# A routed feed-forward stage on one core: the first layer's fp32 product replaced by three fp32r products of high and low parts

## The chip, the cores and the metric

The kernel runs on one core of a Trainium2 chip. The metric is the device time of one execution in microseconds, lower is better. The kernel before took 1937.72 us in the median of 3 runs (1935.43 to 1938.97).

## The reference, cut to what matters

Four layers in a row, each followed by a residual sum and a layer norm: a linear attention, a switch attention, a rotary attention and, last, a feed-forward layer that works on half of the tokens. The change is in the last one alone:

```python
def _L1_ffn_ref(x, w_r, b_r, W1, b1, W2, b2):   # x (4, 1024, 128), W1 (128, 512), W2 (512, 128)
    k = int(0.5 * s)
    weights = (jnp.einsum('bsd,do->bso', x, w_r) + b_r).squeeze(-1)
    top_vals, _ = jax.lax.top_k(weights, k)
    selected = weights > top_vals[:, -1][:, None]
    hidden = jax.nn.gelu(jnp.einsum('bsd,dh->bsh', x, W1) + b1, approximate=False)
    blk = jnp.einsum('bsh,hd->bsd', hidden, W2) + b2
    return jnp.where(selected[..., None], blk, x)
x = _layernorm(x + _L1_ffn_ref(x, ...), axis=-1)
```

## The kernel before

The last stage is `depth_lead`. It works on four batches (b = 0 to 3) of T = 1024 tokens, each with NT = 8 tiles of 128 tokens. HALF is 512 columns, one PSUM bank. Every engine runs a program of its own, in the order in which it is written, and the engines wait for each other by counting semaphores.

TensorE, for each batch, runs `expand(b, 0)`, then `turn_x(b + 1)` (eight transposes of the next batch's x into two banks), `expand(b, 1)`, `router_row(b + 1)` (the router's product, two halves), `expand(b, 2)`, `expand(b, 3)`, `router_column(b + 1)` (eight tiny transposes), and `contract(b)` (the second layer, 32 products of 128 columns). `expand(b, n)` (line 2588, its product on L2594) computes 128 of the 512 hidden units for 1024 tokens. `turn_x(0)`, `router_row(0)` and `router_column(0)` come ahead of the loop.

ScalarE runs `hidden(b, 0)` (the gelu of 1024 columns, L2529), `copy_x(b + 1)` (two copies PSUM to SBUF, L2511), `hidden(b, 1)`, `copy_rows(b + 1)` (L2522), `hidden(b, 2)`, `hidden(b, 3)`, and then `finish_norm(b - 1)` (eight instructions, L2537), which writes the output of the batch before. So the next batch's `hidden(b + 1, 0)` stands behind `finish_norm(b - 1)`.

VectorE runs `choose(0)` and then, for each batch, `choose(b + 1)`, `gather(b, half)` and `moment_stats` for both halves (L2661, L2669), and `moment_guess(b)` (L2678 to L2681). `choose` counts for every token how many have a router weight at least as large: eight passes over 1024 columns (L2641), then `d_sel` and `d_weight` (L2647, L2649). `moment_guess(b)` waits until `finish_norm(b - 1)` has written all its eight tiles (`dve.wait_ge(normed, NT * b)`), since it overwrites the statistics that those read.

GpSimd runs `keep(b + 1)` (three products and sums over 1024 columns, L2474, L2475, L2477, which wait for `d_weight`) and then `inverse_roots(b)` (14 instructions of 8 columns each, L2486 to L2491, which wait for `d_rs` of L2681). ScalarE's `finish_norm(b)` waits for the last of them. Only for the last batch does VectorE do the roots itself (`last_norm`).

SyncE writes each batch's output when its tiles are there. The weights were loaded in the stage before.

Of the kernel before, what the change touches and what calls it, by code (L numbers as in the profile page):

```python
# [11 lines left out]
F32 = mybir.dt.float32  # L12
F32R = mybir.dt.float32r
BF16 = mybir.dt.bfloat16
I32 = mybir.dt.int32
ALU = mybir.AluOpType
# [3 lines left out]
P = 128  # L20
B, T, D = 4, 1024, 128
NT = T // P
HALF = 512
# [2389 lines left out]
def depth_lead(nc, x, out_dram, ps, ident, I, place, signals, past, weights, kept_from, tag):  # L2413

    FF = 512
    NB = FF // P
    K = T // 2
    ctx = ExitStack()
    with ctx:  # L2419
        sb = lambda name, shape, dt=F32: ctx.enter_context(nc.sbuf_tensor(tag + name, shape, dt))  # L2420
        sem = signals.names(tag)
        w1, w2, b1, b2, wr, br = weights.w1, weights.w2, weights.b1, weights.b2, weights.wr, weights.br
        xT = sb("xT", [P, 2, T])
        w_row, w_col, ge = sb("w_row", [P, 2, T]), sb("w_col", [P, 2, NT]), sb("ge", [P, 2, T])
        count, sel, weight = sb("count", [P, NT]), sb("sel", [P, 2, NT]), sb("weight", [P, 2, NT])
        hid = sb("hid", [P, NB, T])
# [5 lines left out]
        assert kept_from is None or nc.sbuf_base <= kept_from  # L2432
        r_in, w1_in, w2_in, b2_in = weights.r_in, weights.w1_in, weights.w2_in, weights.b2_in
        turned, xT_sb, row_ps, row_sb, col_ps, col_sb = map(sem, ("turned", "xT_sb", "row_ps", "row_sb", "col_ps", "col_sb"))
        hid_ps, hid_sb, blk_ps = map(sem, ("hid_ps", "hid_sb", "blk_ps"))
        counts, chosen, scaled, kept_rdy, y_rdy = map(sem, ("counts", "chosen", "scaled", "kept", "y"))
        moments, newton, normed, norm_steps = map(sem, ("moments", "newton", "normed", "norm_steps"))
        out_done = [sem(f"out_done{b}") for b in range(B)]
        piece_b = [ps[:, 0, :], ps[:, 1, :]]
        hid_b = [ps[:, i:i + 2, :].rearrange("p a n -> p (a n)") for i in (2, 4)]  # L2440
# [21 lines left out]
        @block.gpsimd  # L2462
        def _(pool):
            if past is not None:
                past.clear(pool)

            def keep(b):

                if b == 0:
                    pool.wait_ge(b2_in, 16)  # L2470
                pool.wait_ge(chosen, 2 * b + 2)
                if b >= 2:
                    pool.wait_ge(y_rdy, NT * (b - 1))
                nc.gpsimd.tensor_tensor(kept[:, b % 2, :, :], x[:, b * NT:(b + 1) * NT, :], weight[:, b % 2, :].unsqueeze(2).broadcast_to([P, NT, D]), ALU.mult).then_inc(scaled, 1)  # L2474
                nc.gpsimd.tensor_tensor(shifts[:, :, :], b2[:, :].unsqueeze(1).broadcast_to([P, NT, D]), sel[:, b % 2, :].unsqueeze(2).broadcast_to([P, NT, D]), ALU.mult).then_inc(scaled, 1)  # L2475
                pool.wait_ge(scaled, 2 * b + 2)
                nc.gpsimd.tensor_tensor(kept[:, b % 2, :, :], kept[:, b % 2, :, :], shifts[:, :, :], ALU.add).then_inc(kept_rdy, 1)  # L2477
                pool.wait_ge(kept_rdy, b + 1)

            def inverse_roots(b):  # L2480

                pool.wait_ge(moments, MOMENT_STEPS * (b + 1))
                st = Steps(pool, newton, NEWTON_STEPS * b)
                var, half_step = tmp[:, 0, :], tmp[:, 1, :]
                for _ in range(3):
                    st.link(nc.gpsimd.tensor_tensor(half_step, rs[:, :], rs[:, :], ALU.mult))  # L2486
                    st.link(nc.gpsimd.tensor_tensor(half_step, half_step, var, ALU.mult))
                    st.link(nc.gpsimd.tensor_scalar(half_step, half_step, -0.5, 1.5, ALU.mult, ALU.add))
                    st.link(nc.gpsimd.tensor_tensor(rs[:, :], half_step, rs[:, :], ALU.mult))
                st.link(nc.gpsimd.tensor_tensor(shift[:, :], mv[:, :, 0], rs[:, :], ALU.mult))  # L2490
                st.done(nc.gpsimd.tensor_scalar(shift[:, :], shift[:, :], -1.0, None, ALU.mult))  # L2491
                assert st.n == NEWTON_STEPS, st.n

            keep(0)
            for b in range(B):
                if b + 1 < B:
                    keep(b + 1)
                    inverse_roots(b)

        @block.scalar  # L2500
        def _(act):
            nc.scalar.preload_act_table(ACT.Gelu)

            def copy_x(b):

                for half in range(2):
                    act.wait_ge(turned, 2 * b + half + 1)
                    if b >= 2 and half == 0:
                        act.wait_ge(hid_ps, NB * (b - 1))
                    cols = slice(half * HALF, (half + 1) * HALF)  # L2510
                    nc.scalar.copy(xT[:, b % 2, cols], piece_b[half]).then_inc(xT_sb, 1)  # L2511

            def copy_rows(b):

                if b == 0:
                    act.wait_ge(r_in, 16 * 2)
                if b >= 2:
                    act.wait_ge(counts, NT * (b - 1))
                for half in range(2):
                    act.wait_ge(row_ps, 2 * b + half + 1)  # L2520
                    cols = slice(half * HALF, (half + 1) * HALF)
                    nc.scalar.activation(w_row[:, b % 2, cols], piece_b[half], ACT.Identity, bias=br[:, 0:1]).then_inc(row_sb, 1)  # L2522

            def hidden(b, n):

                act.wait_ge(hid_ps, NB * b + n + 1)
                if b and n == 0:
                    act.wait_ge(blk_ps, 2 * b)
                nc.scalar.activation(hid[:, n, :], hid_b[n % 2], ACT.Gelu, bias=b1[:, n:n + 1]).then_inc(hid_sb, 1)  # L2529

            def finish_norm(b):

                act.wait_ge(newton, NEWTON_STEPS * (b + 1))
                if b >= 2:
                    act.wait_ge(out_done[b - 2], 16)
                for t in range(NT):
                    nc.scalar.activation(yo[:, b % 2, t, :], y[:, b % 2, t, :], ACT.Identity, bias=shift[:, t:t + 1], scale=rs[:, t:t + 1]).then_inc(normed, 1)  # L2537

            copy_x(0)
            copy_rows(0)  # L2540
            act.wait_ge(w1_in, 16 * 2)
            for b in range(B):
                hidden(b, 0)
                if b + 1 < B:
                    copy_x(b + 1)
                hidden(b, 1)
                if b + 1 < B:
                    copy_rows(b + 1)
                hidden(b, 2)
                hidden(b, 3)  # L2550
                if b:
                    finish_norm(b - 1)
            act.wait_ge(norm_steps, 10)
            act.wait_ge(out_done[B - 3], 16)
            for t in range(NT // 2, NT):
                nc.scalar.activation(yo[:, (B - 1) % 2, t, :], y[:, (B - 1) % 2, t, :], ACT.Identity, bias=shift[:, t:t + 1], scale=rs[:, t:t + 1]).then_inc(normed, 1)  # L2556

        @block.tensor
        def _(pe):
# [12 lines left out]
            def router_row(b):  # L2572

                if b == 0:
                    pe.wait_ge(r_in, 16 * 2)
                for half in range(2):
                    pe.wait_ge(xT_sb, 2 * b + half + 1)
                    nc.tensor.matmul(piece_b[half], wr[:, :], xT[:, b % 2, half * HALF:(half + 1) * HALF], start=True, stop=True).then_inc(row_ps, 1)  # L2578

            def router_column(b):  # L2580
# [6 lines left out]
            def expand(b, n):  # L2587

                if NB * b + n >= 2:
                    pe.wait_ge(hid_sb, NB * b + n - 1)  # L2590
                if b == 0 and n == 0:
                    pe.wait_ge(w1_in, 16 * 2)
                for s in range(0, T, HALF):
                    last = nc.tensor.matmul(hid_b[n % 2][:, s:s + HALF], w1[:, n * P:(n + 1) * P], xT[:, b % 2, s:s + HALF], start=True, stop=True)  # L2594
                last.then_inc(hid_ps, 1)

            def contract(b):
# [28 lines left out]

        @block.vector
        def _(dve):

            def choose(b):  # L2630

# [52 lines left out]
            def last_norm(b):  # L2684
# [11 lines left out]
                for t in range(NT // 2):  # L2696
                    st.done(nc.vector.tensor_scalar(yo[:, b % 2, t, :], y[:, b % 2, t, :], mv[:, t, 0:1], rs[:, t:t + 1], ALU.subtract, ALU.mult))

            choose(0)
            for b in range(B):  # L2700
                if b + 1 < B:
                    choose(b + 1)
                st = Steps(dve, moments, MOMENT_STEPS * b)
                for half in range(2):
                    gather(b, half)
                    moment_stats(b, st, half)
                moment_guess(b, st)
# [87 lines left out]
def program(nc, I, out_dram):  # L2795
    ctx = ExitStack()
    with ctx:
# [7 lines left out]
        with ExitStack() as held:  # L2805
# [31 lines left out]

            linear.release()
            depth_lead(nc, r3, out_dram, ps, ident, I, nc.Block(), depth, middle, weights, lead.kept_from, "d_")
            middle.release()  # L2840
        redo_all(nc, r1, r2, out_dram, ps, ident, I, depth, flag)
# [81 lines left out]
```

## Time and profile before

| what | value |
|---|---|
| median of 3 runs | 1937.72 us |
| the profiled execution | 1932.66 us, span 1930.9 us |
| last stage | from 1836.8 us to the end of the span |
| TensorE busy | 1739.3 us, 90% of the span |
| VectorE, ScalarE, GpSimd busy | 1136.8, 1274.8, 939.5 us |
| mean granted TensorE clock | 0.966 |

Times in the trace count from the start of the span. "PE" is TensorE's product, "PEld" its weight load, DVE is VectorE, ACT is ScalarE, POOL is GpSimd. A product in plain fp32 appears as two instructions. Ends of products are modelled, so their pace is read from their starts.

### The profile page before, as it was taken

How to read it: one execution, taken by the hardware profiler on the slowest of the kernel's cores; microseconds unless marked ns; L12 is line 12 of the kernel's file. 1: busy time of each engine (PE TensorE's matmuls, PEld its weight loads, DVE VectorE, ACT ScalarE, POOL GpSimd, SP SyncE). 2: the span in 40 equal slices, each digit the busy share in tenths (PEclk: the TensorE clock that was granted, in tenths of full speed). 3: DMA queues.
4: the chain of work that ended last, by engine and by line, in shares of the span. 5: the costliest groups of instructions: out<-in, count | busy, mean ns of one | idle time of the engine just before them, and what ended most of it. 6: DMA issues, size and time to landing. Idle time of an engine off the chain costs nothing. (4 is left out here: it accounts for less than half of the span.)

```text
span 1930.9 us, 25433 instructions
## 1 busy us (share of the span) xinstructions
PE 1739.3 (90%) x8942; PEld 832.9 (43%) x8942; DVE 1136.8 (59%) x1868; ACT 1274.8 (66%) x2447; POOL 939.5 (49%) x566
## 2 busy tenths in 40 slices
PE   7888479999999999999999999879999999998695
PEld 3443345545554445554454555324333333332264
DVE  5888597986668876588766566531423223120286
ACT  2121215766767677767577666768998999999543
POOL 3556206778876778757798678860000000000033
PEclk9999689999999999999999999989999999999898
DMA  2000100000000000000000000130221312201001
GB/s 72 1 1 0 35 11 11 21 21 11 21 11 22 11 21 11 22 11 21 11 22 20 12 11 11 33 131 23 66 88 31 123 40 70 74 36 36 1 12 35
DMA packets 27863, 59.04 MB, mean 31 GB/s; under 512 B 3840, under 2 KB 14800, under 8 KB 27728
## 3 DMA queue, kind: packets, MB, share of 16 engines
q1 hardware_dynamic: 27728, 57.32, 9.2%
q8 instruction: 75, 1.23, 0.3%
q14 instruction: 60, 0.49, 0.1%
HBM read 38.44 MB, written 18.87 MB: 30 GB/s over the span
## 5 line engine op out<-in xcount | busy, mean ns | idle before, releaser
L742 POOL TENSOR_TENSOR b_psum<-b_psum,b_probs 128x1024 f32<-128x1024 f32 x192 | 461.5, 2404 | 181.1 <-ACT b_probs L886 174.9
L2193 ACT ACTIVATE c_probs<-banks 128x1024 f32<-128x1024 f32 x512 | 483.5, 1029 | 46.0 <-PE banks L2242 35.1
L1268 DVE TENSOR_TENSOR b_gated<-banks,b_g 128x480 f32<-128x480 f32 x512 | 314.2, 655 | 229.4 <-PE banks L987 224.5
L886 ACT ACTIVATE b_probs<-banks 128x1024 f32<-128x1024 f32 x256 | 254.0, 1018 | 226.5 <-PE banks L1020 225.7
L987 PE MATMUL banks<-b_w,b_xh 128*128 128x480 f32 x1024 | 353.9, 400 | 32.7 <-DVE b_gated L1268 18.6
L1276 DVE TENSOR_REDUCE b_tok<-b_gated 128x192 f32<-128x960 f32 x256 | 281.3, 1138 | 0.5
L1020 PE MATMUL banks<-b_qq,b_kk 64*128 64x512 f32 x1024 | 262.2, 623 | 10.2 <-DVE b_gated L1268 10.0
L857 ACT ACTIVATE b_share<-b_o,b_picked 128x64 f32<-128x64 f32 x1080 | 268.7, 337 | 1.5 <-DVE b_o L1301 1.5
L1052 PE MATMUL banks<-b_probs,b_tok 128*64 128x512 f32 x1024 | 252.2, 614 | 2.2 <-ACT b_probs L886 2.2
L2257 PE MATMUL banks<-c_probs,c_vg 128*32 128x512 f32 x2048 | 249.4, 605 | 2.9 <-DVEq L2300 2.6
L987 PEld LDWEIGHTS banks<-b_w,b_xh 128*128 128x128 f32 x1024 | 195.2, 191 | 115.6 <-issue 40.0
L2178 POOL COPY c_vg<-c_v 128x64 f32<-128x64 f32 x60 | 12.8, 255 | 424.5 <-PE banks L2257 376.2
L2242 PE MATMUL banks<-c_queries,c_keys 32*128 32x512 f32 x1024 | 193.0, 465 | 27.0 <-ACT c_probs L2193 26.0
L987 PE MATMUL banks<-b_w,b_xl 128*128 128x480 f32 x512 | 196.3, 383 | 0.0
L2242 PEld LDWEIGHTS banks<-c_queries,c_keys 32*128 32x128 f32 x1024 | 79.8, 183 | 195.3 <-ACT c_probs L2193 174.9
L753 POOL TENSOR_TENSOR b_z<-b_z,b_share 128x1280 f32<-128x1280 f32 x54 | 157.5, 2917 | 0.0
L1052 PEld LDWEIGHTS banks<-b_probs,b_tok 128*64 128x64 f32 x1024 | 62.7, 137 | 175.9 <-issue 143.5
L1020 PEld LDWEIGHTS banks<-b_qq,b_kk 64*128 64x128 f32 x1024 | 87.5, 187 | 106.6 <-issue 54.5
L304 POOL TENSOR_TENSOR a_qscan<-a_scan,a_q 128x1024 f32<-128x1024 f32 x36 | 89.9, 2497 | 88.4 <-DVE a_scan L467 88.2
L742 POOL TENSOR_TENSOR b_psum<-b_probs 128x1024 f32<-128x1024 f32 x32 | 76.4, 2387 | 78.1 <-ACT b_probs L886 78.1
L2257 PEld LDWEIGHTS banks<-c_probs,c_vg 128*32 128x32 f32 x2048 | 53.8, 110 | 117.7 <-issue 78.8
L2347 DVE COPY c_acc<-banks 128x512 f32<-128x512 f32 x32 | 22.1, 691 | 138.4 <-PE banks L2257 137.5
(243 smaller groups left out, 1877.0 us busy)
## 6 DMA issues: line engine op xcount, KB each, us to landing
b_raw_w<-in_L_ffn_W SPq DMA_DIRECT2D x32, 480.0 KB, 3.4
c_heads<-c_split SPq DMA_DIRECT2D x24, 512.0 KB
c_keys<-c_heads SPq DMA_DIRECT2D x16, 512.0 KB, 3.6
c_queries<-c_heads SPq DMA_DIRECT2D x16, 512.0 KB, 4.6
c_heads<-c_split SPq DMA_DIRECT2D x8, 384.0 KB
a_xs<-in_L_attn_x SPq DMA_DIRECT2D x4, 512.0 KB, 8.0
out<-d_yo SPq DMA_DIRECT2D x3, 512.0 KB, 3.6
c_heads<-c_split SPq DMA_DIRECT2D x8, 128.0 KB
```

The source lines that it names most:

```text
L742: nc.gpsimd.tensor_tensor(psum[:, par, :], prev, probs[:, i % 4, :], ALU.add).then_inc(psum_rdy, 1)
L753: nc.gpsimd.tensor_tensor(zf, zf, sf, ALU.add).then_inc(z_rdy[half], 1)
L857: nc.scalar.activation(dst[:, e, :], o[:, t, :], ACT.Copy, scale=picked[:, b % 2, t, h * E + e:h * E + e + 1]).then_inc(share_rdy, 1)
L886: nc.scalar.activation(probs[:, i % 4, :], score_b[i % 2], ACT.Exp).then_inc(exp_rdy, 1)
L987: last = nc.tensor.matmul(proj_b[u % WAYS][:, 0:HALF_W], a[:, x_of % 2, t * P:(t + 1) * P], w[:, par, part, j, :], start=(i == 0), stop=(i ...
L1020: last = nc.tensor.matmul(score_b[i % 2][:, lo:hi], kk[rows, par, (side + i) % 2, i // 2 * P:(i // 2 + 1) * P], qq[rows, par, :], start=Tr ...
L1052: last = nc.tensor.matmul(acc_b[DH * half:DH * half + DH, :], tok[:, n % 4, 2, i, :], probs[:, i % 4, lo:hi], start=(i == 0), stop=(i == N ...
L1268: nc.vector.tensor_tensor(shape(gated[:, t % 2, j, :]), shape(proj_b[u % WAYS][:, 0:HALF_W]), g.unsqueeze(2).broadcast_to([P, 3, HD2, E]), ...
L1276: nc.vector.tensor_reduce(tok[:, n % 4, :, t, :].rearrange("p j (f d) -> p f j d", f=2), gated[:, t % 2, :, :].rearrange("p f (j d e) -> p ...
L2193: nc.scalar.activation(probs[:, step % 4, c, :, :], unit_b[u % NU], ACT.Exp, scale=float(HD) ** -0.5).then_inc(exp_rdy, 1)
L2242: last = nc.tensor.matmul(unit_b[u % NU][:, s, :], keys[at:at + 32, par, kt * P:(kt + 1) * P], queries[at:at + 32, par, c * HALF:(c + 1) * ...
L2257: last = nc.tensor.matmul(acc_b[at:at + 32, :], vg[par][:, kt, 2 * pp + s, :], probs[:, kt % 4, half, s, :], start=(kt == 0), stop=(kt == ...
```

## The change

ScalarE makes a second copy of each transposed half, rounded to fp32r (`xh`), behind the plain copy `xT`, which the router and VectorE still use. VectorE makes `xl = xT - xh` in a new step `split_low(b)`, two instructions of 512 columns, ahead of `choose(b)`. The weights are split once: `w1h` by ScalarE ahead of `copy_rows(0)`, `w1l` by GpSimd ahead of `keep(0)`. `expand` does three fp32r products in place of the fp32 one, for each of its two halves. New waits: `router_row` for `x_high`, `expand(b, 0)` for `x_low` (and once for `w_low`), ScalarE's `copy_x(b)` from b = 2 for `x_low` of batch b - 2, `split_low(b)` from b = 2 for the products of batch b - 2.

```diff
+        xh, xl = sb("xh", [P, 2, T], F32R), sb("xl", [P, 2, T], F32R)
+        w1h, w1l = sb("w1h", [P, NB * P], F32R), sb("w1l", [P, NB * P], F32R)
...
+            pool.wait_ge(w_high, 1)
+            nc.gpsimd.tensor_tensor(w1l[:, :], w1[:, :], w1h[:, :].bitcast(F32), ALU.subtract).then_inc(w_low, 1)
             keep(0)
...
                     if b >= 2 and half == 0:
                         act.wait_ge(hid_ps, NB * (b - 1))
+                        act.wait_ge(x_low, 2 * (b - 1))
                     cols = slice(half * HALF, (half + 1) * HALF)
                     nc.scalar.copy(xT[:, b % 2, cols], piece_b[half]).then_inc(xT_sb, 1)
+                    nc.scalar.copy(xh[:, b % 2, cols], piece_b[half]).then_inc(x_high, 1)
...
             copy_x(0)
+            act.wait_ge(w1_in, 16 * 2)
+            nc.scalar.copy(w1h[:, :], w1[:, :]).then_inc(w_high, 1)
             copy_rows(0)
-            act.wait_ge(w1_in, 16 * 2)
...
                     pe.wait_ge(xT_sb, 2 * b + half + 1)
+                    pe.wait_ge(x_high, 2 * b + half + 1)
                     nc.tensor.matmul(piece_b[half], wr[:, :], xT[:, b % 2, half * HALF:(half + 1) * HALF], start=True, stop=True).then_inc(row_ps, 1)
...
                 if b == 0 and n == 0:
-                    pe.wait_ge(w1_in, 16 * 2)
+                    pe.wait_ge(w_low, 1)
+                if n == 0:
+                    pe.wait_ge(x_low, 2 * b + 2)
                 for s in range(0, T, HALF):
-                    last = nc.tensor.matmul(hid_b[n % 2][:, s:s + HALF], w1[:, n * P:(n + 1) * P], xT[:, b % 2, s:s + HALF], start=True, stop=True)
+                    for i, (w, a) in enumerate(((w1h, xh), (w1h, xl), (w1l, xh))):
+                        last = nc.tensor.matmul(hid_b[n % 2][:, s:s + HALF], w[:, n * P:(n + 1) * P], a[:, b % 2, s:s + HALF], start=(i == 0), stop=(i == 2))
...
+            def split_low(b):
+
+                if b >= 2:
+                    dve.wait_ge(hid_ps, NB * (b - 1))
+                for half in range(2):
+                    cols = slice(half * HALF, (half + 1) * HALF)
+                    dve.wait_ge(x_high, 2 * b + half + 1)
+                    nc.vector.tensor_tensor(xl[:, b % 2, cols], xT[:, b % 2, cols], xh[:, b % 2, cols].bitcast(F32), ALU.subtract).then_inc(x_low, 1)
...
+            split_low(0)
             choose(0)
             for b in range(B):
                 if b + 1 < B:
+                    split_low(b + 1)
                     choose(b + 1)
```

## Rows read from the trace of the kernel before

**Rows 1.** The chain of waits, last stage: start, duration, engine, tile, line
```profile
1842.98 1.91 PE banks L2594 x4
1861.31 1.72 PE banks L2594 x4
1897.47 6.88 PE banks L2594 x16
1905.54 7.43 PE banks L2608 x64
1912.99 1.13 DVE d_y L2661 x4
1915.05 0.65 DVE d_mv L2678 x8
```

**Rows 2.** One full batch: busy PE, PEld, DVE, ACT, POOL, granted clock, DMA, GB/s
```profile
1861.15:1879.20 18.05, 17.43 (x102) 12.23 (x101) 16.59 (x46) 9.87 (x16) 8.93 (x17) 1.00 0.05 13
```

**Rows 3.** Timeline of VectorE, last stage: start, duration, ..., idle before and releaser
```profile
1853.14 0.17 DVE L2649 TENSOR_SCALAR d_weight<-d_sel 128x8 f32<-128x8 f32 x1
1853.25 0.17 DVE L2633 COPY d_w_col<-banks 128x8 f32<-128x8 f32 x1
1871.39 0.17 DVE L2633 COPY d_w_col<-banks 128x8 f32<-128x8 f32 x1 [1.19 <-PE banks L2584]
1889.47 0.17 DVE L2633 COPY d_w_col<-banks 128x8 f32<-128x8 f32 x1 [1.29 <-PE banks L2584]
1906.09 0.17 DVE L2681 TENSOR_SCALAR d_rs<-d_tmp 128x8 int32<-128x8 int32 x1
```

**Rows 4.** Timeline of GpSimd, last stage
```profile
1853.47 1.90 POOL L2474 TENSOR_TENSOR d_kept<-c_r,d_weight 128x1024 f32<-128x1024 f32 x1 [98.84 <-DVE d_weight L2649]
1906.40 0.20 POOL L2486 TENSOR_TENSOR d_tmp<-d_rs 128x8 f32<-128x8 f32 x1 [0.38 <-DVE d_rs L2681]
1910.07 0.23 POOL L2491 TENSOR_SCALAR d_shift<-d_shift 128x8 f32<-128x8 f32 x1
```

**Rows 5.** Timeline of ScalarE, last stage
```profile
1838.11 1.31 ACT L2511 COPY d_xT<-banks 128x512 f32<-128x512 f32 x2
1840.78 1.49 ACT L2522 ACTIVATE d_w_row<-banks,c_d_br 128x512 f32<-128x512 f32 x2 [1.37 <-PE banks L2578]
1864.08 1.06 ACT L2511 COPY d_xT<-banks 128x512 f32<-128x512 f32 x2
1892.26 3.19 ACT L2537 ACTIVATE d_yo<-d_y,d_shift,d_rs 128x128 f32<-128x128 f32 x8 [2.26 <-POOL d_shift L2491]
1899.22 1.11 ACT L2529 ACTIVATE d_hid<-banks,c_d_b 128x1024 f32<-128x1024 f32 x1 [3.77 <-PE banks L2594]
1910.34 3.19 ACT L2537 ACTIVATE d_yo<-d_y,d_shift,d_rs 128x128 f32<-128x128 f32 x8 [4.85 <-POOL d_shift L2491]
```

**Rows 6.** Timeline of TensorE, switch attention: fp32r products of 480 columns
```profile
902.20 0.59 PE L987 MATMUL banks<-b_w,b_xh 128*128 128x480 f32 x2
902.63 0.38 PE L987 MATMUL banks<-b_w,b_xl 128*128 128x480 f32 x1
```

**Rows 7.** Timelines, switch attention: a split of x by ScalarE and VectorE
```profile
225.33 1.13 ACT L827 CAST b_xh<-b_xT 128x512 fp32r<-128x512 f32 x2
226.05 1.29 DVE L1213 TENSOR_TENSOR b_xl<-b_xT,b_xh 128x512 fp32r<-128x512 f32 x2 [10.47 <-ACT b_xh L827]
```

**Rows 8.** Timelines of VectorE and GpSimd where both read SBUF
```profile
367.26 3.27 DVE L1232 TENSOR_TENSOR b_beats<-b_gate 128x256 bf16<-128x256 f32 x2
367.33 2.69 POOL L742 TENSOR_TENSOR b_psum<-b_psum,b_probs 128x1024 f32<-128x1024 f32 x1
```

**Rows 9.** Groups by line and shape: GpSimd, whole span and last stage
```profile
L742 POOL TENSOR_TENSOR b_psum<-b_probs 128x1024 f32<-128x1024 f32 x32 | 76.4, 2387 | 78.1 <-ACT b_probs L886 78.1
L2477 POOL TENSOR_TENSOR d_kept<-d_kept,d_shifts 128x1024 f32<-128x1024 f32 x4 | 9.4, 2350 | 0.3
```

**Rows 10.** Stretches and TensorE's timeline around a gap: the granted clock stands behind POOL's busy time
```profile
675.87 1.58 PE L1020 MATMUL banks<-b_qq,b_kk 64*128 64x512 f32 x4 [3.29 <-DVE b_gated L1268]
676.40:679.90 3.50, 3.50 (x10) 0.77 (x8) 1.53 (x2) 2.41 (x8) 1.31 (x1) 0.51 0.00 0
```

More of the change, by code:

```diff
@@ L2434, in depth_lead @@
         turned, xT_sb, row_ps, row_sb, col_ps, col_sb = map(sem, ("turned", "xT_sb", "row_ps", "row_sb", "col_ps", "col_sb"))
+        x_high, x_low, w_high, w_low = map(sem, ("x_high", "x_low", "w_high", "w_low"))
         hid_ps, hid_sb, blk_ps = map(sem, ("hid_ps", "hid_sb", "blk_ps"))
```

## The prediction

> **What bounds the kernel now.** I read the chain of waits first, cut to the last stage, since nothing before it is touched. There the chain runs on TensorE almost without a break: a batch's blocks, then its contraction, one batch after the other, from 1842.98 us to 1912.99 us [rows 1]. Four fp32 instructions of one block (two halves) start 1.72 us apart in all (0.43 us each). Only then does it pass to VectorE, whose last stretch begins with the means of batch 3 at 1915.05 us. That view names a single bound, and it tempts one to price the change by TensorE alone. So I read the stretch of one full batch next: of 18.05 us TensorE is busy 17.43 and VectorE 16.59 [rows 2]. VectorE's own timeline shows what is left: between one batch's `d_rs` and the next `choose` it is idle 1.19 us and 1.29 us, waiting for the router's columns [rows 3]; between batch 0 and batch 1 it is not idle at all (its `d_weight` at 1853.14 is followed by the next copy at 1853.25). VectorE's round is thus only 1.2 us shorter than TensorE's, and the change shortens the one and lengthens the other.
>
> The third reading is what hangs on VectorE's round. When `d_rs` of batch 2 is there at 1906.26, GpSimd runs its 14 root instructions to 1910.30 [rows 4] and ScalarE `finish_norm(2)` from 1910.34 to 1913.53 [rows 5]. `moment_guess(3)` on VectorE waits for exactly that (`normed >= 24`), and begins at 1915.05 because its own statistics came later. So this second path ends 1.52 us ahead of the first; with some 0.07 us for the semaphore, it has 1.45 us of slack.
>
> **TensorE's part.** An fp32r product of 480 columns starts every 0.215 us (902.20 to 902.63 for two) [rows 6]. For 512 columns I take 0.215 to 0.23 us; the weights are loaded alongside there as they will be here. A block goes from 1.72 us to 6 x 0.215 = 1.29 us, so 0.43 us less, 1.7 us in a batch, 6.9 us in all. Part of it goes back at once: the router now waits for both copies of each half. Two copies take 1.06 us [rows 5], four 2.12. In a batch's time, block 0 ends at 1.3, the gelu at 2.6, the four copies at about 4.75; the router's second half starts then, 0.5 us later than TensorE could, and the gelu of block 3 ends at 9.7 (10.8 before). A batch of TensorE becomes about 17.0 us (18.05 before). In the last batch nothing but blocks and gelus is left: gelu 1.11 us plus about 0.3 of hand-over against 1.29 per block and two banks, about 1.4 us per block, 1.5 us less in all. If TensorE alone set the end, the gain would be 3 x 1.0 + 1.5 = 4.5 us.
>
> **VectorE's path, which I take to set the end.** Five terms.
>
> Start. `choose(0)` waits for rows that wait for the router, now behind `xh`. The plain copies end at 1839.42; four take about 1.1 us more, `w1h` 0.55 more (a cast SBUF to SBUF, two in 1.13 us [rows 7]). But the router's products were the late ones: ScalarE was idle 1.37 us for them ahead of the rows [rows 5]. The first half of the router starts 0.5 us later, partly regained as its second pass falls beyond the rise of the clock. I take +0.3 us. Bounds: +0.1 (all hidden) to +1.6 (all three copies in series). The `w1l` subtraction of GpSimd, half of a 2.35 us instruction [rows 9], about 1.2, ends near 1842.4, ahead of the first block; if that cover is gone it costs the first block a few tenths, on TensorE alone. `split_low(0)` lies in VectorE's idle time ahead of `choose(0)`.
>
> `split_low(1)`. Two subtractions of 512 columns take 1.29 us, 0.6 us apart [rows 7]. This pair follows `d_weight` of batch 0 at once, and GpSimd's first `keep` instruction starts 0.22 us after that point (1853.47 against 1853.25) [rows 3, 4]. What happens when a VectorE instruction with two SBUF inputs meets a GpSimd instruction is in the trace: a pair of small comparisons took 3.27 us, while a GpSimd instruction began 0.07 us after the first, took 2.69 us and ended at 370.02, half a microsecond before the pair [rows 8] (it takes 2.39 us in the mean of its like [rows 9]). So the first comparison ran, GpSimd waited for it, then GpSimd ran whole, and only then the second comparison. Here the same gives 0.6 (first half) + 1.9 (GpSimd's product [rows 4]) + 0.6 (second half) = 3.1 us. Bounds: 1.2 (the pair goes through) and 5.0 (GpSimd also gets ahead of the first). I take 3.1, as the row is this very case.
>
> The Trainium skill says the same in "SBUF — State Buffer", section "SBUF: two separate sides": the pair of ports that VectorE and GpSimd share is locked for a whole instruction by whichever starts first, and the other blocks fully. By that rule the first half starts first and the rest depends on who comes next; [rows 8] decide for GpSimd, and read otherwise the rule would leave this term at 1.2.
>
> `split_low(2)` and `split_low(3)` follow `d_rs`, when GpSimd starts its roots, instructions of 0.2 us. Each pair costs 1.2 plus at most one or two such instructions: 1.3 us each (1.2 to 1.6). GpSimd is held up in turn by about 0.7 us, which delays `finish_norm(0)` and `finish_norm(1)`, not `finish_norm(2)`, beside which no split runs.
>
> What comes back: the idle 1.19 and 1.29 us, since the router's columns come earlier than VectorE is ready: 2.5 us.
>
> Sum for `d_rs` of batch 2: 0.3 + 3.1 + 2 x 1.3 - 2.5 = +3.5 us, at 1909.8. Roots and `finish_norm(2)` follow as before, ending at 1917.0; 3.5 less the slack of 1.45 leaves about +2.0 us for the start of the means of batch 3, and behind these nothing changes.
>
> Does TensorE's path stay below? `finish_norm(1)` comes 3.6 + 0.7 us later (1892.26 + 4.3, ending near 1899.8), and the gelu of block 0 of batch 3 is behind it, at 1899.9 (1899.22 before). From there to the contraction 5.4 us (6.3 before): 1905.3, and the statistics of batch 3 end 0.2 us earlier than before, at 1914.8. That is 2.2 us ahead of 1917.0. The contraction's other condition, `gather(2)`, comes at 1900.9 + 3.5 = 1904.4. The `x_low` wait of `expand(b, 0)` is met: `split_low(2)` ends near 1874.9 and `split_low(3)` near 1893.1, against blocks due from 1877.4 and 1895 on.
>
> **Forecast.** The profiled execution took 1932.66 us (span 1930.9); with the sum 1934.7. The median of the runs is 5.1 us above the profiled one, and I add the sum to the median: 1939.7 us. All 6.9 us that TensorE is spared go into waiting.
>
> **Rivals.** (A) The pair of `split_low(1)` is not parted by GpSimd: 0.3 + 1.2 + 2.5 - 2.5 - 1.45 = 0, so 1937.7. For it: each of the second halves is ready to issue before the first ends. Against: the parted pair in [rows 8]. Chance 0.22.
>
> (B) TensorE's path sets the end after all and gains 4.5 us: 1933.2. It needs VectorE's path not to lengthen; the wait for `normed` stands in the code and its slack is 1.45 us, and even without any port wait this path eats it. Chance 0.04.
>
> (C) TensorE's clock. In batch 2 the copies stand behind a `finish_norm(0)` that ends near 1881, so TensorE waits some 3 us for the router. After a gap of 3.29 us the trace shows 3.5 us at a granted clock of 0.51, the level of 1.2 GHz [rows 10]. Such a fall in batch 2 costs 1.7 us, mostly covered by ScalarE's lateness; a second that meets the contraction of batch 3 (7.4 us at full clock [rows 1]) costs 1.7 to 7.4 more. It decides once the contraction ends over 2.2 us late: at 5 us late the time is 1942.5, with the contraction wholly at half clock 1944.9. For it: the waits grow. Against: ahead of the last contraction I see no gap of that length, and at gaps of 0.7 us the clock stayed at 1.00 [rows 2]. Chance 0.12.
>
> My forecast has 0.62. A difference of 0.2%, 3.9 us, is about what a measurement of this kernel can tell from no change. Faster by more: 0.04, case B. Slower by more: C, and the upper end of the forecast (a start near 1.6 or a parted first half), 0.16. The same: 0.80. By the bounds the path gives -0.3 (0.1 + 1.2 + 2.4 - 2.5 - 1.45) to +5.9 us (1.6 + 5.0 + 3.2 - 2.5 - 1.45); cutting the far end and allowing 1.5 us for the scatter of medians, the range is 1936.0 to 1943.0.
>
> **What would show each step.** In the profile after: fp32r starts 0.21 to 0.23 us apart; the first subtraction of `split_low(1)` about 0.7 us and the second about 2.4, with a `keep` instruction between; VectorE without idle time before `choose(2)` and `choose(3)`; the means of batch 3 released by ScalarE's `d_yo` and not by the statistics; idle time of TensorE before the router's product. If the chain of waits still runs over the contraction of batch 3, the sum is wrong in its main choice; if the second subtraction takes 0.7 us, it is rival A.

## The result and the profile after

Timed in 20 runs each, the changed kernel takes 1940.08 us in the median (1934.61 to 1947.31) and the kernel before 1936.20 (1931.16 to 1941.36); the ratio is 1.0022, 95% interval 1.0012 to 1.0032. By that ratio it is slower by 4.3 us (2.3 to 6.2); the medians differ by 3.9. A second set of 11 runs, beside 34 of the kernel before, gave 1.0027 (1.0017 to 1.0036). The forecast was 1939.7 us within 1936 to 1943.

The stages ahead of the last one are the same instructions in every kernel here, yet in the 14 profiles the last one begins anywhere between 1834.70 and 1846.56 us after the start of the span. Ahead of it TensorE had its low clock for 105.7 us in the earliest profile and for 129.4 us in the latest. So the mechanism is read inside the last stage, counted from ScalarE's table load, which begins it (1839.18 us in the profile after). From there to the end it took 94.05 and 94.25 us in two profiles of the kernel before, 97.85 and 97.78 us in two of the changed one: +3.7 us.

The chain of waits of the changed kernel, last stage: start, duration, engine, tile, line. (The dots stand for lines that are left out.)

```profile
1841.70 3.77 PE banks L2587 x4
...
1847.48 9.70 DVE d_ge L2662 x16
...
1858.09 2.38 DVE d_xl L2649
1860.58 9.70 DVE d_ge L2662 x16
...
1875.31 1.74 DVE d_tmp L2701
1877.15 0.48 DVE d_xl L2649
...
1916.59 0.20 POOL d_shift L2493
...
1917.54 2.79 ACT d_yo L2544 x7
1920.45 0.31 DVE d_mv L2699 x3
```

Where [rows 1] showed a TensorE that never left the chain, the chain now enters VectorE with the first `choose` and stays there until the `d_rs` of batch 2, goes over GpSimd's roots and ScalarE's `finish_norm(2)`, and comes back to VectorE at the means of batch 3. No contraction is on it.

VectorE's timeline of the same kernel, which answers to [rows 3]:

```profile
1847.28 0.17 DVE L2654 COPY d_w_col<-banks 128x8 f32<-128x8 f32 x1 [4.02 <-PE banks L2593]
...
1857.48 2.99 DVE L2649 TENSOR_TENSOR d_xl<-d_xT,d_xh 128x512 fp32r<-128x512 f32 x2
1860.40 0.15 DVE L2654 COPY d_w_col<-banks 128x8 f32<-128x8 f32 x1
...
1877.15 1.30 DVE L2649 TENSOR_TENSOR d_xl<-d_xT,d_xh 128x512 fp32r<-128x512 f32 x2
1878.37 0.15 DVE L2654 COPY d_w_col<-banks 128x8 f32<-128x8 f32 x1
...
1896.28 0.15 DVE L2654 COPY d_w_col<-banks 128x8 f32<-128x8 f32 x1
...
1912.89 0.17 DVE L2702 TENSOR_SCALAR d_rs<-d_tmp 128x8 int32<-128x8 int32 x1
...
1920.45 0.88 DVE L2699 BATCH_NORM_AGGREGATE d_mv<-d_stats 128x2 f32<-128x6 f32 x8 [2.62 <-ACT d_yo L2544]
```

The idle times ahead of the copies of batches 2 and 3 are gone, and a new one of 2.62 us stands ahead of the means, put down to ScalarE's `d_yo`: the wait for `normed`. GpSimd's and ScalarE's timelines, which answer to [rows 4, 5]:

```profile
1857.72 2.20 POOL L2477 TENSOR_TENSOR d_kept<-c_r,d_weight 128x1024 f32<-128x1024 f32 x1 [13.34 <-DVE d_weight L2670]
1859.89 2.34 POOL L2478 TENSOR_TENSOR d_shifts<-c_d_b,d_sel 128x1024 f32<-128x1024 f32 x1
```

```profile
1899.87 3.19 ACT L2544 ACTIVATE d_yo<-d_y,d_shift,d_rs 128x128 f32<-128x128 f32 x8 [6.64 <-POOL d_shift L2494]
1902.97 2.10 ACT L2536 ACTIVATE d_hid<-banks,c_d_b 128x1024 f32<-128x1024 f32 x2
1917.14 3.18 ACT L2544 ACTIVATE d_yo<-d_y,d_shift,d_rs 128x128 f32<-128x128 f32 x8 [8.85 <-POOL d_shift L2494]
```

And here is what the products cost, in TensorE's timeline. Their starts are 0.23 us apart.

```profile
1891.01 0.39 PE L2606 MATMUL banks<-d_xh,d_w1l 128*128 128x512 f32 x1
1891.24 0.39 PE L2606 MATMUL banks<-d_xh,d_w1h 128*128 128x512 f32 x1
1891.46 0.39 PE L2606 MATMUL banks<-d_xl,d_w1h 128*128 128x512 f32 x1
1891.69 0.39 PE L2606 MATMUL banks<-d_xh,d_w1l 128*128 128x512 f32 x1
```

### The profile page after: what moved, and what is told of

Its sections match the earlier page's. It is cut to its first block and busy times, and to the rows that moved or that the text cites. A ratio compares the mean times of both kernels' runs of the same rounds, so it can differ in the third digit from the quotient of the medians.

```text
span 1937.0 us, 25527 instructions
## 1 busy us (share of the span) xinstructions
PE 1736.7 (90%) x8974; PEld 839.8 (43%) x8974; DVE 1147.6 (59%) x1876; ACT 1278.2 (66%) x2456; POOL 943.3 (49%) x567
```

## The experiments

All marks are in us from the start of the last stage, one profile each. "Rise" is when TensorE's granted clock goes from 1.2 to 2.4 GHz, "copy 0" VectorE's first column copy, "copy 1" the second, "rs 2" the guess of the roots of batch 2, "means 3" the first mean of batch 3. "End" is the end of the span. The ratio is to the kernel before, timed beside it.

| kernel | rise | copy 0 | copy 1 | rs 2 | means 3 | end | ratio (95%) |
|---|---|---|---|---|---|---|---|
| before | 3.55 | 6.20 | 16.44 | 69.28 | 78.24 | 94.05 | |
| e12_before_again | 3.88 | 6.37 | 16.61 | 69.44 | 78.41 | 94.25 | 1.0012 (0.9986 to 1.0039) |
| after | 10.89 | 8.09 | 21.21 | 73.71 | 81.27 | 97.85 | 1.0022 (1.0012 to 1.0032) |
| e10_after_again | 6.42 | 7.74 | 20.85 | 73.37 | 80.93 | 97.78 | 1.0027 (1.0017 to 1.0036) |
| e1_high_from_copy | 3.55 | 6.20 | 19.33 | 71.84 | 79.42 | 95.90 | 1.0044 (1.0027 to 1.0061) |
| e8_high_from_copy_again | 3.71 | 6.28 | 19.41 | 71.91 | 79.47 | 96.27 | 1.0018 (1.0006 to 1.0031) |
| e2_low_before_weight | 6.87 | 7.74 | 19.15 | 71.81 | 79.40 | 96.08 | 1.0018 (1.0008 to 1.0029) |
| e3_double_stats | 6.96 | 7.74 | 20.86 | 73.41 | 79.13 | 95.56 | 1.0007 (0.9993 to 1.0020) |
| e4_all_three | 3.91 | 6.39 | 17.80 | 70.46 | 75.44 | 91.78 | 0.9984 (0.9967 to 1.0001) |
| e11_all_three_again | 3.86 | 6.36 | 17.78 | 70.44 | 75.41 | 92.21 | 0.9990 (0.9981 to 1.0000) |
| e5_before_double_stats | 6.29 | 7.24 | 17.48 | 70.32 | 79.29 | 95.49 | 0.9994 (0.9979 to 1.0009) |
| e6_no_low_of_x | 14.01 | 8.08 | 19.81 | 70.65 | 78.39 | 94.98 | 1.0005 (0.9988 to 1.0022) |
| e7_split_fp32_products | 13.94 | 8.09 | 21.26 | 74.13 | 83.11 | 99.81 | 1.0026 (1.0007 to 1.0046) |
| e9_roots_on_gpsimd | 3.96 | 6.40 | 17.82 | | 74.30 | 89.54 | 0.9972 (0.9961 to 0.9984) |

The kernel before, timed against itself, came out at 1.0012 (0.9986 to 1.0039). So a ratio alone does not carry a microsecond here, while the marks of two profiles of one kernel agree within 0.4 us, and only the rise moves further.

**The late start.** `e1_high_from_copy` makes `xh` from `xT` instead of from PSUM, so the router's product waits for the plain copies alone, as before the change:

```diff
                     nc.scalar.copy(xT[:, b % 2, cols], piece_b[half]).then_inc(xT_sb, 1)
-                    nc.scalar.copy(xh[:, b % 2, cols], piece_b[half]).then_inc(x_high, 1)
+                for half in range(2):
+                    act.wait_ge(xT_sb, 2 * b + half + 1)
+                    cols = slice(half * HALF, (half + 1) * HALF)
+                    nc.scalar.copy(xh[:, b % 2, cols], xT[:, b % 2, cols]).then_inc(x_high, 1)
...
-                    pe.wait_ge(x_high, 2 * b + half + 1)
```

> xh is made from xT in SBUF, behind both plain copies, so the router's product no longer waits for it. Times below count from the start of the stage (ScalarE's table load). Theory (the 0.5 us gap ahead of the first router product let TensorE's clock rise late, 10.8 us into the stage instead of 3.6): the rise is back near 3.6 us, VectorE's first column copy starts at about 6.5 us (8.10 in the changed kernel, 6.20 before), and the means of batch 3 start 1.4 to 1.7 us earlier. Rival (the time of the rise has nothing to do with that gap): the copy starts near 7.6 and the means 0.5 us earlier. Whole time about 1.6 us under the changed kernel, some 2 us over the one before.

Copy 0 is back at 6.20 us and the means come 1.85 us earlier. In TensorE's timeline of this kernel the router follows the transposes at once and takes 2.71 us as before:

```profile
1834.74 1.94 PE L2580 MATMUL banks<-ident,c_r 128*128 128x128 f32 x8 [8.02 <-PEq L2837]
1836.72 2.71 PE L2589 MATMUL banks<-d_xT,c_d_wr 128*128 128x512 f32 x4
```

In the changed kernel it waits 0.53 us for `d_xh` and then takes 3.75:

```profile
1839.22 1.94 PE L2577 MATMUL banks<-ident,c_r 128*128 128x128 f32 x8 [8.01 <-PEq L2835]
1841.70 3.75 PE L2587 MATMUL banks<-d_xT,c_d_wr 128*128 128x512 f32 x4 [0.53 <-ACT d_xh L2518]
```

The busy times of two stretches of the changed kernel show why: the granted clock (third from the end) was 0.50, the level of 1.2 GHz, for the whole start of the stage, and 1.00 behind it.

```profile
1839.20:1850.00 10.80, 9.47 (x27) 5.84 (x28) 4.08 (x8) 5.21 (x8) 1.26 (x1) 0.50 0.00 0
1850.00:1865.60 15.60, 14.88 (x103) 12.39 (x102) 15.50 (x26) 7.45 (x10) 6.88 (x3) 1.00 0.00 1
```

The 1.9 us by which copy 0 is late in the changed kernel are thus 0.5 us of waiting, 1.05 us of the router's slower passes and 0.36 us of the eight tiny transposes behind the rows, which took 1.02 us where they took 0.66 before. But the timed runs of e1 came out long: their median was 1943.54 us, 7.4 us above the kernel before, and the profiled run was the shortest of the five. So it ran again, beside the changed kernel itself.

> The same kernel as e1_high_from_copy, whose profile had the stage 1.95 us shorter than the changed kernel's while its timed runs were 7 us above the kernel before. Theory (the timed runs were scatter from the stages ahead, where the clock falls at other places in every execution): 1 to 2 us over the kernel before and 1 to 3 under the changed kernel of the same call; the clock's rise again between 3.5 and 6.5 us into the stage. Rival (the edit costs something that its profile did not show): again more than 4 us over the kernel before.

> The changed kernel unaltered, beside the others on the same chip, and with a second profile. Theory (the router's wait for xh lets the clock rise late): the rise lies again later than 6.5 us into the stage, the first column copy at 7.7 us or later, the means of batch 3 at 80.9 to 81.3. Rival (the late rise was chance): rise near 3.6 us and first column copy near 6.7.

> The kernel before, unaltered, for a second profile of the same start. Theory (without the wait for xh the clock rises early): the rise within 6.5 us of the stage's start, the first column copy at 6.2 to 7.3 us, the means of batch 3 at 78.2 to 79.3. Rival (the time of the rise is chance in either kernel): a rise at 6.9 us or later and a first column copy at 7.7 or later.

The marks of e8 repeat those of e1 within 0.1 us, but for the rise (0.2 us) and the end (0.4 us). In time the expectation for e8 failed: it was 3.7 us over the kernel before and not 1 to 2, and only 0.6 us under the changed kernel timed beside it. Its ratio of 1.0018 and the 1.0027 of the changed kernel cannot be told apart, so the gain of this edit is shown inside the stage alone (96.27 us against 97.78). The 1.0044 of e1 was not met again. The four long runs of e1 had a mean granted clock of 0.960 to 0.963, against 0.967 in the profiled one; what lowered it is not known. Of the expectation for e10, the number 6.5 us for the rise failed by 0.1 (6.42), copy 0 and the means came as written. For e12 all three numbers did. Over all profiles: where the router waits for `xh` (after, e10, e2, e3, e6, e7) the rise lies at 6.42 to 14.01 us and copy 0 at 7.74 to 8.09; where it does not (the other eight) the rise lies at 3.55 to 3.96 and once at 6.29, and copy 0 at 6.20 to 6.40 and once at 7.24. The rise is not fixed in either group. That the gap of half a microsecond delays it is the likeliest reading of 14 profiles, and e5 shows that a late rise also comes without the gap. With nearly the same rise (6.29 us in e5, 6.42 in e10) copy 0 differs by 0.50 us, which is the wait alone; the rest of the late start comes from the clock.

**The parted pair.** `e2_low_before_weight` puts `split_low(1)` ahead of the instructions that release GpSimd:

```diff
                     dve.wait_ge(scaled, 2 * (b - 1))
+                if b == 0:
+                    split_low(1)
                 nc.vector.tensor_scalar(sel[:, b % 2, :], count[:, :], float(K), None, ALU.is_lt).then_inc(chosen, 1)
...
                 if b + 1 < B:
-                    split_low(b + 1)
+                    if b:
+                        split_low(b + 1)
                     choose(b + 1)
```

> split_low(1) stands ahead of d_sel and d_weight of batch 0, so GpSimd has not yet been released. Theory (the shared port parts the pair): its second subtraction takes 0.7 us instead of 2.4, the pair costs 1.2 us instead of 2.9, and the means of batch 3 start 1.6 to 1.8 us earlier than in the changed kernel. Rival (the 2.9 us has another source, such as the copy it reads): nothing changes. Whole time about 1.7 us under the changed kernel.

VectorE's timeline of this kernel:

```profile
1852.53 1.29 DVE L2649 TENSOR_TENSOR d_xl<-d_xT,d_xh 128x512 fp32r<-128x512 f32 x2
1853.74 0.17 DVE L2670 TENSOR_SCALAR d_sel<-d_count 128x8 f32<-128x8 f32 x1
```

The pair takes 1.29 us instead of 2.99. GpSimd's first product, released only now, takes 1.90 us instead of 2.20:

```profile
1854.27 1.90 POOL L2477 TENSOR_TENSOR d_kept<-c_r,d_weight 128x1024 f32<-128x1024 f32 x1 [14.19 <-DVE d_weight L2672]
```

From copy 0 to copy 1 it is 11.41 us, 13.12 in the changed kernel: 1.71 us. Of these 1.5 us arrive at the means, which come 1.87 us earlier, 0.35 of it by the start. GpSimd's product between the two subtractions is the cause of the 2.38 us. The durations fit the exclusive use that the forecast priced: GpSimd's product waited 0.3 us for the first subtraction, and the second subtraction waited for the whole product.

**The wait for the norm.** `e3_double_stats` gives `mv`, `rs`, `shift` and `tmp` two buffers, indexed by `b % 2`:

```diff
-                if b:
-                    dve.wait_ge(newton, NEWTON_STEPS * b)
-                    dve.wait_ge(normed, NT * b)
+                if b >= 2:
+                    dve.wait_ge(newton, NEWTON_STEPS * (b - 1))
+                    dve.wait_ge(normed, NT * (b - 1))
                 for t in range(NT):
-                    st.done(nc.vector.bn_aggr(mv[:, t, :], stats[:, t, :]))
+                    st.done(nc.vector.bn_aggr(mv[:, b % 2, t, :], stats[:, t, :]))
```

> mean, root, shift and scratch have two buffers, so moment_guess(b) waits for the norm of batch b - 2 instead of b - 1. Theory (in the changed kernel the end hangs on finish_norm(2)): the means of batch 3 start right behind the statistics, 2.5 us earlier than in the changed kernel, and the chain of waits runs over the contraction of batch 3 again. Rival (the contraction comes as late anyway): less than 0.5 us. Whole time 2.5 us under the changed kernel, about 1.4 over the one before.

`e5_before_double_stats` is the same edit on the kernel before.

> The kernel before, with two buffers for the statistics. Theory (there the wait for finish_norm(2) had 1.5 us of slack): no change, within 0.3 us in the stage. Rival (that wait costs in both kernels): up to 2.5 us faster.

In e3 the means stand right behind the statistics. They come 2.1 us earlier (1.8 counted from copy 0), and the chain of waits again runs over the contraction, directly behind batch 2's:

```profile
1891.19 7.41 PE banks L2620 x64
1898.60 5.66 PE banks L2606 x24
1904.28 1.12 ACT d_hid L2536
1905.45 7.42 PE banks L2620 x64
...
1914.97 0.65 DVE d_mv L2699 x8
```

In e5 copy 0 came 1.04 us later than before (a late rise) and the means 1.05 us later: the edit itself gives nothing there. The wait costs only where the change made it late. In e3 the forecast's rival C also showed itself. TensorE waited 1.96 us for `xh` in batch 2, behind a late `finish_norm(0)`, and the clock fell. The four router instructions took 3.60 us, and the granted clock of the stretch was 0.60:

```profile
1883.60 3.60 PE L2587 MATMUL banks<-d_xT,c_d_wr 128*128 128x512 f32 x4 [1.96 <-ACT d_xh L2518]
```

```profile
1884.00:1888.00 4.00, 4.00 (x8) 1.81 (x7) 3.88 (x16) 2.81 (x4) 2.93 (x2) 0.60 0.08 22
```

The wait alone does not decide it. In e10 the same wait was 1.89 us, and in e1 and e8 (for `xT`) 2.04 us, and there the clock did not fall:

```profile
1886.13 2.06 PE L2587 MATMUL banks<-d_xT,c_d_wr 128*128 128x512 f32 x4 [1.89 <-ACT d_xh L2518]
```

The contraction of batch 3 starts at 69.6 us in e3, 0.8 us later than in e10, which has the same copy 0: that is what is missing to the 2.5 us expected.

**All three.** `e4_all_three` joins the edits of e1, e2 and e3.

> All three edits. Theory: the means of batch 3 then start where the contraction of batch 3 lets them. VectorE's d_rs of batch 2 comes about 1.1 us later than before the change, gather(2) likewise, the contraction of batch 3 starts near 66 us into the stage (68.7 before), and the means of batch 3 at about 75.5 us (78.24 before, 81.27 in the changed kernel): 2.5 us faster than the kernel before. Rival (the three are one cost seen three times): no more than the best of them alone, some 2.5 us under the changed kernel and over the one before.

> The same kernel as e4_all_three, timed in more rounds, to tell it from the kernel before. Theory: 2.5 us (0.13%) faster than before, in the stage 2.0 to 3.0 us shorter. Rival (its gain was scatter): no difference within 0.5 us.

The means came at 75.44 and 75.41 us, 2.8 and 3.0 us ahead of the two profiles before, and the stage is 1.8 to 2.5 us shorter. In time they gave 0.9984 and 0.9990, just at the edge of what can be told from 1 (2.0 us in the medians of e11, 2.5 expected). Counted from the changed kernel the edits add up roughly: 1.85, 1.5 and 1.8 (the last two without the start, which e1 has) make 5.15 us, and 5.83 were found. The rival, one cost seen three times, is refuted.

**TensorE's side.** In `e6_no_low_of_x` nothing subtracts, the waits for `x_low` are gone or wait for `x_high`, and the second product takes `xh` once more, so its result leaves out the low part of x:

```diff
-                    for i, (w, a) in enumerate(((w1h, xh), (w1h, xl), (w1l, xh))):
+                    for i, (w, a) in enumerate(((w1h, xh), (w1h, xh), (w1l, xh))):
```

> The changed kernel without VectorE's subtractions: the second product takes xh again in place of xl, so the low part of x is left out of the result; all else stands. Theory (VectorE's extra work and the late first column copy are all that stands against the cheaper products): the start stays 1.9 us late, the rest of TensorE's path gains 3 x 0.9 + 1.5 us, and the means of batch 3 start 1.5 to 2.5 us earlier than before the change, 5 us earlier than in the changed kernel. Rival (VectorE's round was as long as TensorE's anyway): the end is VectorE's round again, about +1.9 - 2.5 - 1.5, which is 0 to 2 us under the kernel before.

In `e7_split_fp32_products` all splits and waits stay and the product is the old one:

```diff
-                    for i, (w, a) in enumerate(((w1h, xh), (w1h, xl), (w1l, xh))):
-                        last = nc.tensor.matmul(hid_b[n % 2][:, s:s + HALF], w[:, n * P:(n + 1) * P], a[:, b % 2, s:s + HALF], start=(i == 0), stop=(i == 2))
+                    last = nc.tensor.matmul(hid_b[n % 2][:, s:s + HALF], w1[:, n * P:(n + 1) * P], xT[:, b % 2, s:s + HALF], start=True, stop=True)
```

> The changed kernel with all its splits and waits, but the product itself stays the plain fp32 one. Theory (VectorE's path sets the end, not TensorE): TensorE's products are 6 us longer in sum, yet less than 1.5 us of it shows against the changed kernel. Rival (TensorE's path would set the end but for the cheaper products): 3 to 5 us slower than the changed kernel.

Both had the latest rise of all, at 14 us. e6 did not do what I wrote: its means came at 78.39, as before the change, 2.9 us ahead of the changed kernel's and not 5. Its chain of waits runs over TensorE, so the mechanism holds, but the start took more than 1.9 us: copy 0 is 1.9 us late, and copy 1 another 1.5 (11.73 us behind copy 0, 10.24 before), since the first blocks ran at 1.2 GHz. Contraction 0 starts 3.4 us later than before, and the 3.2 us that TensorE gains from there to contraction 3 only make up for that. From contraction 0 to 1 and from 1 to 2 it is 17.05 and 17.08 us (18.05 and 18.08 before), the 1.0 us per batch of the forecast.

e7 has its means at 83.11, 1.84 us behind the changed kernel's, a little over my 1.5, and its chain runs over TensorE:

```profile
1912.07 6.88 PE banks L2605 x16
1918.98 1.12 ACT d_hid L2536
1920.14 7.43 PE banks L2619 x64
...
1929.66 0.65 DVE d_mv L2698 x8
```

`finish_norm(2)` ended at 81.56 there, so VectorE's path alone would have given about 81.7, an estimate from that end and the 0.13 us that follow it in the changed kernel. The cheaper products are thus worth 1.4 to 1.8 us inside the changed kernel, after such a start: with the old ones TensorE bounds it, with the new ones VectorE does. After an earlier rise the old products would come earlier too, and what the new ones are worth then was not run.

**A version that beats both.** A wait for GpSimd costs VectorE something in the kernel before too. `d_tmp` (8 columns, 0.17 us in the last batch, beside no `keep`) takes 1.74 us, until GpSimd's last `keep` instruction has ended:

```profile
1868.26 1.74 DVE L2680 TENSOR_SCALAR d_tmp<-d_mv 128x8 f32<-128x8 f32 x1
1867.62 2.35 POOL L2477 TENSOR_TENSOR d_kept<-d_kept,d_shifts 128x1024 f32<-128x1024 f32 x1
```

On top of e4, `e9_roots_on_gpsimd` moves these two instructions to GpSimd, and the splits of batches 2 and 3 into the middle of `choose`:

```diff
+                st.link(nc.gpsimd.tensor_scalar(var, mv[:, b % 2, :, 1], LN_EPS, None, ALU.add))
+                st.link(nc.gpsimd.tensor_scalar(rs[:, b % 2, :].bitcast(I32), var.bitcast(I32), -0.5, float(0x5F3759DF), ALU.mult, ALU.add))
                 for _ in range(3):
...
                 for t in range(NT):
+                    if t == 2 and b >= 2:
+                        split_low(b)
```

(VectorE makes the two for the last batch alone.)

> On top of e4_all_three: d_tmp and d_rs of batches 0 to 2 are made by GpSimd instead of VectorE, where d_tmp stood 1.6 us for GpSimd's last keep instruction, and split_low(2) and split_low(3) stand behind the second pass of choose(2) and choose(3). Theory (the port wait of d_tmp is 1.4 us of VectorE's round): the column copies of choose(2) and choose(3) come 17.0 us apart instead of 17.9, TensorE's path is the bound, and the means of batch 3 start near 74.3 us into the stage (75.44 in e4): about 1 us faster than e4. Rival (another VectorE instruction stands there for the port): the spacing stays near 17.9 and nothing is gained.

The means come at 74.30 us, as written. The copies of batches 2 and 3 are 17.2 us apart, the latter with 1.14 us of idle time ahead of it, put down to the router's columns. The chain of waits is TensorE's again:

```profile
1889.53 1.12 ACT d_hid L2541
1890.70 7.41 PE banks L2624 x64
1898.11 5.64 PE banks L2610 x24
1903.78 1.12 ACT d_hid L2541
1904.94 7.43 PE banks L2624 x64
```

Time: 1930.03 us, 1936.22 before, ratio 0.9972 (0.9961 to 0.9984), the only one here clearly under the kernel before. Of the 4.5 us by which its stage is shorter, 3.9 lie ahead of the means; the other 0.6 lie in the tail behind them, whose cause is open. Which of its two edits does how much was not separated.

## Why the prediction was right

The mechanism was as forecast, and the time of 1940.08 us lies 0.4 us from the forecast 1939.7. That closeness is partly luck. The forecast was 2.0 us of added path on a base of 1937.72 us, the median of 3 runs; over 20 runs the kernel before takes 1936.20, 1.5 us less. The change itself cost 3.9 to 4.3 us, about twice what the sum said. Two terms were too small, the start and the stretch behind the means, and smaller errors the other way hid part of that.

**Start.** Taken as +0.3 us, bounds 0.1 to 1.6; found +1.9, outside the bounds, and, in the second pair of profiles, +1.4. This is the term that was mis-sized most. I priced the wait as a shift of half a microsecond and reckoned that the clock would rise when it had before. In all six profiles with that wait it rose only behind the router. The router's passes then start 0.85 us apart to the last, where before the change the last of them started 0.43 us apart.

**`split_low(1)`.** Taken as 3.1, found 2.88 (copy 0 to copy 1: 13.12 and 13.11, before 10.24), and e2 shows the cause. The first subtraction took 0.68 us and the second 2.38, with GpSimd's product between them.

**`split_low(2)`, `split_low(3)`.** Taken as 1.3 each, found 1.22 from the first subtraction to the next copy. The first starts 0.08 us behind the start of `d_rs`, so from `d_rs` to the next copy it is 1.30 us, where the sum amounts to 1.47. GpSimd's first two root instructions beside them took 0.5 us each instead of 0.2, 0.6 us in all where the forecast said 0.7.

**What came back, and the slack.** Both idle times before the column copies are gone. `d_rs` of batch 2 came +4.4 us (+3.9 in the second pair) where +3.5 was written. The start was 1.6 us (1.1) over its term, and the rest of VectorE's path 0.7 us under its terms (+2.5 where +3.2 was written), which hid part of it. Less the slack of 1.5 us, which e5 confirms to be slack, the means of batch 3 came +3.0 and +2.5 us, forecast +2.0.

**Behind the means** I said that nothing changes. The stage grew by another 0.8 us there, and by 1.0 in the second pair. Of this 0.24 lie between the first mean and the last `d_yo`, as the eight means take 0.88 us instead of 0.64 when they follow the wait for the norm (also in e10). The other 0.5 and 0.8 lie between the last `d_yo` and the end of the output, a stretch that took 10.98 to 12.54 us over the kernels here, from the start of that `d_yo`. Its cause stays open.

**TensorE's path.** A batch of 17.0 us was forecast and 17.05 to 17.08 found, in e6 and, from contraction 0 to 1, in the changed kernel; from contraction 1 to 2, where the router waited for `xh` behind a late `finish_norm(0)`, it was 17.7 us there and 19.0 in e10. An fp32r product takes 0.23 us, the upper end of my estimate. The 6.9 us to be spared were reckoned with the lower end, 0.215; at 0.23 a block saves 0.34 us and all sixteen 5.4. This changes nothing here, as it goes into waiting. The contraction of batch 3 was forecast 0.2 us earlier than before; it started at 69.16 us (68.73 before) and, in e10, at 68.85 (68.89).

**Rivals.** A is refuted by the 2.38 us of the second subtraction. B is refuted by the chain; e4 and e9 show what it needed. C happened, in e3, as a single fall in batch 2, and did not reach the end by more than 0.8 us. The wait ahead of it was 2.0 us and not 3, and three profiles with such a wait (e1, e8, e10) had no fall. The measured difference of 0.22% lies on the border of 0.2% that I drew between the same and slower, to which I gave 0.80 and 0.16. The start that I put at 0.3 us deserved more weight on slower.

## What to carry to other kernels

When an engine is sped up and another gets work for it, read the other's idle time round by round before pricing the gain. VectorE had 1.2 and 1.3 us to give in two rounds, and the pairs of 1.2 us vanished in them; in the round from batch 0 to batch 1 it had none, and there the pair cost its full 2.9 us. Place a VectorE instruction with two SBUF operands where GpSimd is idle, not right behind the one that releases it; the same pair cost 1.29 or 2.99 us by its place in the program. Where TensorE starts a stage at its low clock, an added wait of half a microsecond there can cost more than itself: 1.4 to 1.9 us here.

## What was not expected

The moment at which TensorE's clock returned to 2.4 GHz after the start of the stage lay between 3.55 and 14.01 us in 14 profiles, for the same first instructions at 3.55, 3.88 and 6.29 (the start of before) and at 6.42, 6.87, 6.96 and 10.89 (that of after). In e6 and e7, whose first instructions are those of after up to the first block, it lay at 14.01 and 13.94. What decides within a group was not tried.

GpSimd's two `keep` products took 2.20 and 2.34 us beside the subtractions and 1.90 us elsewhere: GpSimd waits for VectorE as well, 0.3 and 0.4 us here.
